# The output product of an attention and expert layer from 16-bit halves, and a new order of its neighbours

## Chip, core and metric

The kernel runs on one core of a Trainium2 chip, in one launch. The metric is the device time of that core in microseconds (us), the median of several runs.

## What is computed

For each of 16 sequences of 256 tokens and width 128, the reference adds three things: the input, a state-space branch and an attention and expert branch. Cut to what matters:

```python
xn = layernorm(x)
# branch 1: xf = depthwise_conv(xn); dt = sigmoid(xf @ dt_w.T + dt_b) * 0.099 + 0.001
#           s_t = exp(dt * A) * s_(t-1) + dt * xf * b;  y_t = sum_d s_t * c      (16 states per channel)
# branch 2:
h = layernorm(xn, ln_g, ln_b)
q, k, v = h @ Wq, h @ Wk, h @ Wv                      # 16 heads of 64
q, k = l2norm(q) * q_scale, l2norm(k) * k_scale
attn = softmax(causal(10 * q @ k.T))
out = concat_heads(attn @ v) @ Wo                     # (256 x 1024) @ (1024 x 128)
h = layernorm(out, ln_g, ln_b)
gate = softmax(h @ gate_w + gate_b)
moe = sum_e gate[e] * (gelu(h @ w1[e] + b1[e]) @ w2[e] + b2[e])      # 8 experts, 512 wide
result = x + y + layernorm(moe, ln_g, ln_b)
```

## The kernel before, in words

All engines run hand-written programs that are fixed when the kernel is built; semaphores join them. After a prologue (weights loaded and split, sequence 0 projected) each engine runs `body(i)` for the sequences i = 0 to 15, then a tail. A body has two halves.

**Pair steps k = 0 to 9.** The 16 heads go as 8 pairs p. TensorE forms the scores of pair k into the PSUM tile S2 (`scores`, L427), ScalarE takes their exponentials (`exps`, L716), GpSimd cuts the causal part (`select`, L875), and one step later TensorE weighs the values (`weigh` of pair k-1, L444) into the PSUM bank O[p % 2]. One more step later VectorE divides (`divide` of pair k-2: L1052, L1055), TensorE turns the quotient in the same bank (`turn_o`, L451), and at step k ScalarE copies the turned pair k-3 to `OT` (`copy_ot`, L722), which frees the bank: `weigh` waits for it by the semaphore `ot_done`. Beside that TensorE projects the next sequence's Q and K from 16-bit halves (`project`, three 512-column products L332 to L334 into a bank J; `project_v` in steps 8 and 9), ScalarE copies and squares them (L666, L668), VectorE sums the squares (L992) and runs the recurrence of branch 1 (`scan` L1148, `add_state` L1158), whose decays ScalarE makes (L728).

**Expert steps m = 0 to 9.** TensorE forms the output product (`output`, L460, float32: the turned pairs as stationary, Wo as moving operand), the experts of the sequence before (`expert_up`, L521 to L523 from 16-bit halves; `expert_down`, L539), turns the next sequence's Q and K (`turn_qk`, L369), whose high halves ScalarE writes (`high`, L689 to L693) and whose low halves VectorE (`low`, L1029 to L1034), and forms scores a first time for their maxima (`scores_for_max`, L387 and L391, into S2 too), which VectorE reduces (`maxima`, L1046). The maxima of four pairs at a time are turned (`turn_max`, L405) and copied (`copy_max`, L697), and `scores(i, 0)` waits for that copy. The gate of the sequence before is turned (L499) and copied (L1106) in step 1, in front of `gated_b2` (L505).

Each engine takes its instructions in the order of its program. That order is written out in the loops of `body`, by the step at which a helper is called; small tables (`TURN_AT`, `MAX_AT`, `O_AT`, `STATES`) say which part comes at which step. `WS` is 64: 16-bit halves of weights are of the weight times 64, and the copy of a result divides by it.

Of the kernel before, what the change touches and what calls it, by code (L numbers as in the profile page):

```python
# [14 lines left out]
P = 128  # L15
# [25 lines left out]
def build(nc, x, a_log, b, c, dt_w, dt_b, conv_w, conv_b, ln_g, ln_b, Wq, Wk, Wv, q_scale, k_scale,  # L41
          Wo, gate_w, gate_b, w1, b1, w2, b2, out):
    ctx = ExitStack()
    with ctx:
# [3 lines left out]
        def sem(name):  # L48
# [13 lines left out]
        wos = sb("wos", [P, HD // P, D])  # L62
# [59 lines left out]
        OT = sb("OT", [P, NP, SEQ])  # L122
# [44 lines left out]
        W132 = hid[:, :, :, :].rearrange("p r c n -> p (r c n)")  # L167
        sel32 = P32[:, :, :, :].rearrange("p r a n -> p (r a n)")[:, 0:8 * P].rearrange("p (h k) -> p h k", h=8)
# [14 lines left out]
            st_ready ex_done sel_done pv_done rr_done on_done ot_ready ot_done  # L183
# [10 lines left out]
         st_ready, ex_done, sel_done, pv_done, rr_done, on_done, ot_ready, ot_done,  # L194
# [121 lines left out]
        def _(pe):  # L316
# [137 lines left out]
            def output(s):  # L454

                pe.wait_ge(ot_done, (s + 1) * NP)
                pe.wait_ge(ex_done, (s + 1) * NP)
                for t in range(T):
                    for m in range(HD // P):
                        last = mm(S2[:, 0, t * P:(t + 1) * P], OT[:, m, t * P:(t + 1) * P],  # L460
                                  wos[:, m, :], start=(m == 0), stop=(m == HD // P - 1))
                last.then_inc(wo_ready, 1)
# [85 lines left out]
            def prologue():  # L548
# [28 lines left out]
                pe.wait_ge(d_wo, 16)  # L577

            def body(i, older, old, new, newer):
                for k in range(NP + 2):  # L580
                    if k < NP:
                        scores(i, k)
                    if k == 0:
                        turn_max(i, 1)
                    if 1 <= k <= NP:
                        weigh(i, k - 1, older)
                    if new and k < NP:
                        project(i + 1, k)
# [13 lines left out]
                for m in range(NE + 2):  # L602
# [18 lines left out]
                    if not new and m == 8:  # L621
                        turn_gate(i, 0)
                        expert_up(i, 0)
                    if old and 1 <= m <= NE:
# [7 lines left out]
                    if new and m == 8:  # L632
                        turn_max(i + 1, 0)
# [15 lines left out]
        def _(act):  # L649
# [53 lines left out]
            def copy_output(s):  # L703
                act.wait_ge(wo_ready, s + 1)
                from_one(act, o_tr, s)
                fn(z2[:, :, :].rearrange("p t d -> p (t d)"), S2[:, 0, 0:SEQ], ACT.Copy).then_inc(wo_copied, 1)
# [11 lines left out]
            def copy_ot(s, p):  # L718
# [3 lines left out]
                fn(OT[:, p, :], O[p % 2][:, 0:SEQ], ACT.Copy).then_inc(ot_done, 1)  # L722
# [23 lines left out]
            def prologue():  # L746
# [32 lines left out]
                for n in range(NL):  # L779
                    high(0, n)  # L780
                    if n in (1, 5):
                        copy_v(0, n // 4 * 2)
                        copy_v(0, n // 4 * 2 + 1)
                act.wait_ge(setup_vec, 4)
                with_gelu_and_tanh()
                step_tanh(0)
                with_exp_and_ln()
                copy_max(0, 0)

            def body(i, older, old, new, newer):  # L790
                for k in range(NP + 2):
                    if k >= 3:
# [5 lines left out]
                    if new and 1 <= k <= NP:  # L798
                        copy_raw(i + 1, k - 1)
                    if k < NP:  # L800
# [15 lines left out]
                for m in range(NE + 2):  # L816
# [17 lines left out]
                    if new and m == 9:  # L834
                        copy_max(i + 1, 0)
                if new:
                    with_exp_and_ln()

# [101 lines left out]
        def _(dve):  # L940
# [54 lines left out]
            def norm_step(s, half, n):  # L995
# [196 lines left out]
            def prologue():  # L1192
# [64 lines left out]
                for n in range(7, 10):  # L1257
                    g_step(1, n)
                step_inputs(0, 0)
# [14 lines left out]
            STATES = {0: (6,), 1: (7,), 2: (8, 9)}  # L1274

            def body(i, older, old, new, newer):
                for k in range(NP + 2):
                    if k >= 2:
# [28 lines left out]
                for m in range(NE + 2):  # L1307
                    if old and m == 2:
                        o_step(i - 1, 15)
                    if old and m >= 2:  # L1310
                        add_expert(i - 1, m - 2)
                    if new and m == 0:
                        scan(i, 6)
                        low(i + 1, 0)
                        low(i + 1, 1)
                        norm_step(i + 1, 1, 1)
                        norm_step(i + 1, 1, 2)
                        norm_step(i + 1, 1, 3)
                        add_state(i, 6)
                    elif 2 <= m <= NE:  # L1320
                        for d in STATES.get(m, (m + 7,)):
                            scan(i, d)
                            add_state(i, d)
# [3 lines left out]
                    if old and m == 1:  # L1327
                        o_step(i - 1, 14)
# [3 lines left out]
                    if m == 1:  # L1332
                        if not new:
                            scan(i, 6)
# [62 lines left out]
```

## Time and profile before

| | |
|---|---|
| median of 3 runs | 1180.96 us (1180.76 to 1180.98) |
| the profiled execution | 1181.25 us, of which its span is 1179.5 us |
| granted TensorE clock, mean over the span | 0.977 |
| chain that ended last | PE 77%, ACT 12%, DVE 6%, issue 4% |
| busy share of GpSimd | 23% |

PE is TensorE's products and PEld its weight loads, DVE is VectorE, ACT ScalarE, POOL GpSimd. Times in a timeline are us from the span's start, first the start and then the duration, with the count of records in a row; a float32 product leaves two records. Products overlap, so the duration of one is longer than the distance from its start to the next one's. A wait is idle time of an engine, with the instruction that ended it; a wait for several things is put down to the last. A group's mean is over instructions of one shape.

### The profile page before, as it was taken

The page shows a single profiled execution, that of the slowest core. Times are in us where ns is not written, and L with a number is a line of the kernel's source. Part 1 is how long each engine was busy: PE and PEld are TensorE (multiplying, and loading weights), DVE is VectorE, ACT ScalarE, POOL GpSimd, SP SyncE. Part 2 cuts the span into 40 slices and gives each one's busy share as a digit, 9 for nine tenths or more (in the row PEclk, how much of TensorE's full clock was granted, in tenths as well). Part 3 has the DMA queues.
Part 4 walks back from the last instruction along what each step waited for, and adds up shares of the span by engine and source line. Part 5 has one row for each costly group of instructions (what it writes and reads, how often), then busy time and mean ns, then how long its engine had stood idle before and what let it go on. Part 6 is the DMA issues. An engine that isn't in the chain of part 4 may idle for free.

```text
span 1179.5 us, 27543 instructions
## 1 busy us (share of the span) xinstructions
PE 1106.3 (94%) x10435; PEld 920.3 (78%) x10435; DVE 960.0 (81%) x2576; ACT 784.9 (67%) x1772; POOL 268.3 (23%) x324
## 2 busy tenths in 40 slices
PE   4885999999999999999999999999999999999997
PEld 1563788887878888787887878788787888878897
DVE  7779778797987879788797988879798787978773
ACT  5582867758486675858667586766848677584753
POOL 2040312313041231313214041221404123130200
PEclk9795999999999999999999999999999999999999
DMA  6001000000000000000000000000000000000000
GB/s 201 6 1 41 6 1 15 2 11 6 6 11 1 15 2 6 10 6 11 1 15 2 6 10 6 11 1 13 4 6 11 1 15 1 7 6 1 10 2 9
DMA packets 18722, 14.60 MB, mean 12 GB/s; under 512 B 2408, under 2 KB 16160, under 8 KB 18592
## 3 DMA queue, kind: packets, MB, share of 16 engines
q1 hardware_dynamic: 17680, 12.76, 3.6%
q8 instruction: 84, 1.38, 0.5%
q14 instruction: 46, 0.38, 0.1%
q10 hardware_dynamic: 912, 0.09, 0.1%
HBM read 10.75 MB, written 2.10 MB: 11 GB/s over the span
## 4 chain that ended last, share of the span: by engine, by line
PE 77%; ACT 12%; DVE 6%; issue 4%; POOL 0%; POOLq 0%; DVEq 0%; ACTq 0%
PE O L539 18%; PE O L444 14%; PE S L427 9%; PE U L522 4%; PE U L523 4%; PE U L521 4%; PE J L332 3%; PE J L334 3%; PE J L333 3%; PE J L369 3%; PE S L391 3%; PE S L387 2%; PE O L451 2%; ACT L656 2%; ACT hid L743 1%
## 5 line engine op out<-in xcount | busy, mean ns | idle before, releaser
L743 ACT ACTIVATE hid<-U,b1c 128x256 f32<-128x256 f32 x512 | 200.5, 474 | 180.7 <-PE U L523 180.5
L539 PE MATMUL O<-w2s,hid 128*128 128x128 f32 x2048 | 251.8, 276 | 0.0
L539 PEld LDWEIGHTS O<-w2s,hid 128*128 128x128 f32 x2048 | 238.6, 192 | 2.9
L444 PE MATMUL O<-Vx,P 128*128 128x66 f32 x1536 | 198.9, 280 | 16.6 <-ACT OT L722 16.6
L444 PEld LDWEIGHTS O<-Vx,P 128*128 128x128 f32 x1536 | 182.0, 192 | 33.2 <-issue 19.6
L1148 DVE TENSOR_TENSOR_SCAN st<-aexp,u 128x256 f32<-128x256 f32 x256 | 175.2, 684 | 2.3 <-ACT aexp L728 2.3
L867 POOL TENSOR_TENSOR raw<-raw,nr 128x512 f32<-128x512 f32 x120 | 124.6, 1062 | 136.3 <-DVE nr L1011 136.2
L875 POOL TENSOR_SCALAR_AFFINE_SELECT P<-P 128x512 f32<-128x512 f32 x128 | 87.6, 684 | 217.8 <-ACT P L716 217.8
L522 PE MATMUL U<-h2l,w1h 128*128 128x256 f16 x480 | 130.9, 273 | 0.0
L521 PE MATMUL U<-h2h,w1h 128*128 128x256 f16 x480 | 130.9, 273 | 0.0
L523 PE MATMUL U<-h2h,w1l 128*128 128x256 f16 x480 | 130.9, 273 | 0.0
L716 ACT ACTIVATE P<-S 128x768 f32<-128x768 f32 x128 | 103.6, 810 | 36.7 <-PE S L427 36.5
L1046 DVE TENSOR_REDUCE mxn<-S 128x2 f32<-128x256 f32 x248 | 125.8, 550 | 0.1
L855 POOL TENSOR_TENSOR orr<-ove,minus_half 128x2 f32<-128x2 f32 x16 | 11.2, 698 | 495.9 <-DVE ove L1069 495.9
L1158 DVE SCALAR_TENSOR_TENSOR y<-st,bc,y 128x256 f32<-128x256 f32 x240 | 116.9, 487 | 8.3 <-issue 0.3
L728 ACT ACTIVATE aexp<-dt,negA 128x256 f32<-128x256 f32 x256 | 116.9, 516 | 0.0
L1119 DVE SCALAR_TENSOR_TENSOR acc<-O,gate,acc 128x128 f32<-128x128 f32 x240 | 72.9, 345 | 31.3 <-PE O L539 29.3
L992 DVE TENSOR_REDUCE ssq<-sq 128x8 f32<-128x512 f32 x128 | 86.5, 676 | 1.6 <-ACT sq L668 1.6
L1029 DVE SCALAR_TENSOR_TENSOR QTl<-J,wcol,QTh 128x256 f16<-128x256 f32 x64 | 30.8, 481 | 65.7 <-ACT QTh L690 65.6
L666 ACT ACTIVATE raw<-J 128x512 f32<-128x512 f32 x128 | 76.2, 595 | 4.2 <-PE J L334 4.1
L668 ACT ACTIVATE sq<-J 128x512 f32<-128x512 f32 x128 | 77.7, 607 | 0.0
L369 PE MATMUL J<-ident,raw 128*128 128x128 f32 x512 | 70.6, 282 | 7.0 <-DVE QTl L1031 3.7
(193 smaller groups left out, 2153.3 us busy)
## 6 DMA issues: line engine op xcount, KB each, us to landing
xin<-in_L_attn_x SPq DMA_DIRECT2D x16, 128.0 KB, 2.1
xres<-in_L_attn_x SPq DMA_DIRECT2D x16, 128.0 KB, 2.1
hid<-in_L_ffn_w SPq DMA_DIRECT2D x2, 1024.0 KB, 6.4
out_dram<-fin SPq DMA_DIRECT2D x16, 128.0 KB, 1.8
raw<-in_L_ffn_Wq SPq DMA_DIRECT2D x1, 512.0 KB, 4.2
raw<-in_L_ffn_Wk SPq DMA_DIRECT2D x1, 512.0 KB, 6.3
raw<-in_L_ffn_Wv SPq DMA_DIRECT2D x1, 512.0 KB, 7.3
wos<-in_L_ffn_Wo SPq DMA_DIRECT2D x1, 512.0 KB, 11.2
```

Of the source, the lines that this page charges most:

```text
L427: last = mm(S2[:, a, kb * SEQ:kb * P + SEQ], keys, queries, start=(n == 0), stop=(n == 3), skip_group_check=True)
L444: last = mm(dst, P32[:, p % 3, a, c0:c0 + P], Vx[:, kb, 2 * p + a, :], start=(kb == 0), stop=(kb == t))
L521: mm(dst, w1h[:, f:f + P], hi[:, :], start=True, stop=False)
L522: mm(dst, w1h[:, f:f + P], lo[:, :], start=False, stop=False)
L523: last = mm(dst, w1l[:, f:f + P], hi[:, :], start=False, stop=True)
L539: last = mm(O[e % 2][:, t * P:(t + 1) * P], hid[:, e % 2, m, t * P:(t + 1) * P], w2s[:, e * FC + m, :], start=(m == 0), stop=(m == FC - 1))
L728: fn(aexp[:, d, :], dt[:, :], ACT.Exp, scale=negA[:, d:d + 1]).then_inc(a_done, 1)
L743: fn(hid[:, e % 2, f % FC, :], U[q % 2][:, m * SEQ:(m + 1) * SEQ], ACT.Gelu_apprx_tanh, bias=b1c[:, f:f + 1], scale=1.0 / WS).then_inc(gel ...
L867: nc.gpsimd.tensor_tensor(group, group, nr[:, j * 8:(j + 1) * 8].unsqueeze(2).broadcast_to([P, 8, DH]), ALU.mult).then_inc(unit, 1)
L1046: V.tensor_reduce(mxn[:, t, g, hh:hh + DH + 2:DH + 1], max_bank(s, p)[:, :, t * P:(2 * t + 1) * P], AX.X, ALU.max, negate=True).then_inc(m ...
L1148: V.tensor_tensor_scan(st[:, d % 2, :], aexp[:, d, :], u[:, :], 0.0, ALU.mult, ALU.add).then_inc(scan_done, 1)
L1158: V.scalar_tensor_tensor(y[:, s % 2, :], st[:, d % 2, :], bc[:, d:d + 1], y[:, s % 2, :], ALU.mult, ALU.add).then_inc(y_done, 1)
```

## The change

1. **The output product from halves.** `woh` and `wol` are 16-bit high and low halves of Wo times 64, made in the prologue from a float32 copy that is loaded into a part of `P32`; ScalarE writes the high half, VectorE the low one, and the first `copy_max` waits for it. `OT` becomes `OTh` and `OTl`: ScalarE's `copy_ot` writes the high half (semaphore `ot_hi`), and a new VectorE helper `low_o` writes the low half from the bank and the high half and raises `ot_done`. `output` forms three 16-bit products where one float32 product was; `copy_output` divides by 64.
2. **`project` in front of `weigh`** in pair steps 1 to 7.
3. **ScalarE's copy of pair 5** moves from step 8 to step 7, in front of the decays.
4. **`turn_max(i + 1, 0)`** moves in front of the last `expert_down`, and its copy behind the load of the table of exponentials.
5. **VectorE's order.** `low_o` stands first in pair steps 3 to 9, and for pair 7 first in expert step 0. States 6 and 7 are both in expert step 0, in front of the low halves of Q and K, state 8 in step 1, 9 in step 2. The copy of the turned gate in step 1 moves in front of the low halves.

```diff
...
-        wos = sb("wos", [P, HD // P, D])
+        woh = sb("woh", [P, HD // P, D], F16)
+        wol = sb("wol", [P, HD // P, D], F16)
...
-        OT = sb("OT", [P, NP, SEQ])
+        OTh = sb("OTh", [P, NP, SEQ], F16)
+        OTl = sb("OTl", [P, NP, SEQ], F16)
...
+        wos = P32[:, :, :, :].rearrange("p r a n -> p (r a n)")[:, 1024:1024 + HD].rearrange("p (c n) -> p c n", n=D)
...
                 for t in range(T):
+                    dst, q = S2[:, 0, t * P:(t + 1) * P], slice(t * P, (t + 1) * P)
                     for m in range(HD // P):
-                        last = mm(S2[:, 0, t * P:(t + 1) * P], OT[:, m, t * P:(t + 1) * P],
-                                  wos[:, m, :], start=(m == 0), stop=(m == HD // P - 1))
+                        mm(dst, OTh[:, m, q], woh[:, m, :], start=(m == 0), stop=False)
+                        mm(dst, OTh[:, m, q], wol[:, m, :], start=False, stop=False)
+                        last = mm(dst, OTl[:, m, q], woh[:, m, :], start=False, stop=(m == HD // P - 1))
...
+                    if new and k < NP:
+                        project(i + 1, k)
                     if 1 <= k <= NP:
                         weigh(i, k - 1, older)
-                    if new and k < NP:
-                        project(i + 1, k)
...
+                    if new and m == 8:
+                        turn_max(i + 1, 0)
                     if old and 1 <= m <= NE:
                         expert_down(i - 1, m - 1, (i + 1) * NP)
...
-                    if new and m == 8:
-                        turn_max(i + 1, 0)
...
-                fn(OT[:, p, :], O[p % 2][:, 0:SEQ], ACT.Copy).then_inc(ot_done, 1)
+                fn(OTh[:, p, :], O[p % 2][:, 0:SEQ], ACT.Copy).then_inc(ot_hi, 1)
...
+                act.wait_ge(wo_low, 1)
                 copy_max(0, 0)
...
-                    if k >= 3:
+                    if k >= 3 and k != NP:
                         copy_ot(i, k - 3)
...
+                    if k == NP - 1:
+
+                        copy_ot(i, NP - 3)
                     if k < NP:
                         decay(i, 2 * k)
                         decay(i, 2 * k + 1)
...
-                    if new and m == 9:
-                        copy_max(i + 1, 0)
                 if new:
                     with_exp_and_ln()
+                    copy_max(i + 1, 0)
...
+            def low_o(s, p):
+
+                dve.wait_ge(ot_hi, s * NP + p + 1)
+                if p == 0:
+                    from_one(dve, wo_ready, s)
+                V.tensor_tensor(OTl[:, p, :], O[p % 2][:, 0:SEQ], OTh[:, p, :], ALU.subtract).then_inc(ot_done, 1)
...
+                dve.wait_ge(wo_high, 1)
+                V.scalar_tensor_tensor(wol[:, :, :], wos, WS, woh[:, :, :], ALU.mult, ALU.subtract).then_inc(wo_low, 1)
                 step_inputs(0, 0)
...
                 for k in range(NP + 2):
+                    if k >= 3:
+                        low_o(i, k - 3)
                     if k >= 2:
                         divide(i, k - 2)
...
+                    if m == 0:
+                        low_o(i, NP - 1)
+                        for d in (6, 7):
+                            scan(i, d)
+                            add_state(i, d)
...
+                    if old and m == 1:
+                        o_step(i - 1, 14)
                     if new and m > 0 and m in TURN_AT:
                         low(i + 1, TURN_AT[m])
                         low(i + 1, TURN_AT[m] + 1)
-                    if old and m == 1:
-                        o_step(i - 1, 14)
```

How the instructions stand now. VectorE, pair step 6 and the head of step 7, before (st and y are a scan and its state, gl the gate's logits):

```order
L1052 RECIPROCAL rr<-O 128x4 [waits pv_done]
L1055 TENSOR_TENSOR On<-O,rr 128x256 [waits ot_ready,rr_done]
L992 TENSOR_REDUCE ssq<-sq 128x8 [waits qk_raw]
L1148 SCALAR_TENSOR_TENSOR st<-aexp,u 128x256 [waits y_done,a_done]
L1158 SCALAR_TENSOR_TENSOR y<-st,bc,y 128x256 [waits y_done,scan_done]
...
L1094 TENSOR_SCALAR gl<-gl,gm 128x8 [waits o_vec]
L1094 TENSOR_SCALAR gl<-gl,gm 128x8
L1052 RECIPROCAL rr<-O 128x4 [waits pv_done]
L1055 TENSOR_TENSOR On<-O,rr 128x256 [waits ot_ready,rr_done]
```

and after the change:

```order
L1030 TENSOR_TENSOR OTl<-O,OTh 128x256 [waits ot_hi]
L1070 RECIPROCAL rr<-O 128x4 [waits pv_done]
L1073 TENSOR_TENSOR On<-O,rr 128x256 [waits ot_ready,rr_done]
L1003 TENSOR_REDUCE ssq<-sq 128x8 [waits qk_raw]
L1166 SCALAR_TENSOR_TENSOR st<-aexp,u 128x256 [waits y_done,a_done]
L1176 SCALAR_TENSOR_TENSOR y<-st,bc,y 128x256 [waits y_done,scan_done]
...
L1112 TENSOR_SCALAR gl<-gl,gm 128x8 [waits o_vec]
L1112 TENSOR_SCALAR gl<-gl,gm 128x8
L1030 TENSOR_TENSOR OTl<-O,OTh 128x256 [waits ot_hi]
L1070 RECIPROCAL rr<-O 128x4 [waits pv_done]
L1073 TENSOR_TENSOR On<-O,rr 128x256 [waits ot_ready,rr_done]
```

The subtraction that waits for `ot_hi` stands in front of the division; the rest of the step is as it was.

TensorE, from the last scores of a pair step to the turn, before:

```order
L427 MATMUL S<-QTh,KTl 128x128 x2
L444 MATMUL O<-Vx,P 128x66 [waits ot_done,sel_done]
L444 MATMUL O<-Vx,P 128x66 x5
L332 MATMUL J<-wh,hTh 128x512 [waits qk_raw]
L333 MATMUL J<-wh,hTl 128x512
L334 MATMUL J<-wl,hTh 128x512
```

and after:

```order
L430 MATMUL S<-QTh,KTh 128x128 x2
L430 MATMUL S<-QTl,KTh 128x128 x2
L430 MATMUL S<-QTh,KTl 128x128 x2
L335 MATMUL J<-wh,hTh 128x512 [waits qk_raw]
L336 MATMUL J<-wh,hTl 128x512
L337 MATMUL J<-wl,hTh 128x512
L447 MATMUL O<-Vx,P 128x66 [waits ot_done,sel_done]
```

The projection stands between the scores and the weighing, with its wait for the bank J; the weighing is directly in front of the turn.

ScalarE, the end of step 7 and step 8, before:

```order
L668 ACTIVATE sq<-J 128x512 [waits qk_sum]
L728 ACTIVATE aexp<-dt,negA 128x256 x2
L711 ACTIVATE ge,gs<-gl 128x8 [waits o_vec]
L711 ACTIVATE ge,gs<-gl 128x8
L722 ACTIVATE OT<-O 128x256 [waits ot_ready]
L666 ACTIVATE raw<-J 128x512 [waits qk_ready]
```

and after:

```order
L673 ACTIVATE sq<-J 128x512 [waits qk_sum]
L728 ACTIVATE OTh<-O 128x256 [waits ot_ready]
L734 ACTIVATE aexp<-dt,negA 128x256 x2
L717 ACTIVATE ge,gs<-gl 128x8 [waits o_vec]
L717 ACTIVATE ge,gs<-gl 128x8
L671 ACTIVATE raw<-J 128x512 [waits qk_ready]
```

The copy of pair 5 now stands in front of the decays and of the gate's exponentials.

## Rows read from the trace of the kernel before

**Rows 1.** The page, part 1: busy us (share) xinstructions of each engine.

```profile
...
PE 1106.3 (94%) x10435; PEld 920.3 (78%) x10435; DVE 960.0 (81%) x2576; ACT 784.9 (67%) x1772; POOL 268.3 (23%) x324
...
```

**Rows 2.** TensorE's waits: engine, line, waited for: us in total, times, longest us.

```profile
...
PE O L444 <- ACT OT L722: 16.6, 17, 1.1
PE S L387 <- DVE mxn L1046: 11.4, 6, 3.1
...
PE S L427 <- ACT mT L697: 8.5, 15, 0.6
...
PE O L505 <- DVE gateT L1106: 2.8, 14, 0.2
...
```

**Rows 3.** Timeline, TensorE, output: start us, us, line, op, xcount.

```profile
...
708.17 3.74 PE L460 MATMUL S<-wos,OT 128*128 128x128 f32 x32
...
713.21 0.40 PE L391 MATMUL S<-maskb,identb 128*128 128x128 bf16 x4
713.44 0.27 PE L521 MATMUL U<-h2h,w1h 128*128 128x256 f16 x1
...
```

**Rows 4.** Timeline, TensorE, pair steps 7 to 9 of the same body.

```profile
...
697.97 0.22 PE L427 MATMUL S<-QTh,KTl 64*128 64x128 f16 x2
698.12 1.55 PE L444 MATMUL O<-Vx,P 128*128 128x66 f32 x12
699.51 0.38 PE L332 MATMUL J<-wh,hTh 128*128 128x512 f16 x1
...
700.16 0.38 PE L451 MATMUL O<-ident,On 128*128 128x128 f32 x2
701.60 1.52 PE L444 MATMUL O<-Vx,P 128*128 128x66 f32 x12 [1.06 <-ACT OT L722]
...
704.26 0.38 PE L451 MATMUL O<-ident,On 128*128 128x128 f32 x2
...
705.77 0.38 PE L451 MATMUL O<-ident,On 128*128 128x128 f32 x2
...
```

**Rows 5.** Timeline, ScalarE, copies of turned pairs 3, 5 and 6.

```profile
...
694.53 0.36 ACT L722 ACTIVATE OT<-O 128x256 f32<-128x256 f32 x1
...
701.08 0.38 ACT L722 ACTIVATE OT<-O 128x256 f32<-128x256 f32 x1
...
704.95 0.38 ACT L722 ACTIVATE OT<-O 128x256 f32<-128x256 f32 x1
...
```

**Rows 6.** Timeline, VectorE, pair step 6 to the first low parts.

```profile
...
693.05 0.18 DVE L1052 RECIPROCAL rr<-O 128x4 f32<-128x4 f32 x1 [0.22 <-PE O L444]
...
696.28 1.35 DVE L1094 TENSOR_SCALAR gl<-gl,gm 128x8 f32<-128x8 f32 x2
697.55 0.17 DVE L1052 RECIPROCAL rr<-O 128x4 f32<-128x4 f32 x1
...
703.16 0.18 DVE L1052 RECIPROCAL rr<-O 128x4 f32<-128x4 f32 x1
...
705.65 0.68 DVE L1148 TENSOR_TENSOR_SCAN st<-aexp,u 128x256 f32<-128x256 f32 x1
708.81 0.48 DVE L1029 SCALAR_TENSOR_TENSOR QTl<-J,wcol,QTh 128x256 f16<-128x256 f32 x1 [2.48 <-ACT QTh L690]
...
```

**Rows 7.** Timeline, GpSimd, pair step 6.

```profile
...
696.57 2.04 POOL L867 TENSOR_TENSOR raw<-raw,nr 128x512 f32<-128x512 f32 x2
...
```

**Rows 8.** Groups by line and shape: out<-in shapes xcount | busy us, mean ns.

```profile
...
L1158 DVE SCALAR_TENSOR_TENSOR y<-st,bc,y 128x256 f32<-128x256 f32 x240 | 116.9, 487 | 8.3 <-issue 0.3
...
L988 DVE TENSOR_TENSOR hTl<-hT,hTh 128x256 f16<-128x256 f32 x16 | 6.6, 416 | 0.1
...
L1213 DVE SCALAR_TENSOR_TENSOR wl<-raw,wh 128x1024 f16<-128x1024 f32 x3 | 3.6, 1215 | 0.0
...
```

**Rows 9.** Timeline, TensorE, the edge between two bodies.

```profile
...
675.19 0.38 PE L405 MATMUL J<-ident,mxn 128*128 128x128 f32 x2
676.14 0.29 PE L427 MATMUL S<-mT,sel 64*128 64x256 bf16 x2 [0.56 <-ACT mT L697]
...
```

More of the change, by code:

```diff
@@ L182, in build @@
             m_ready mx_done mt_ready mt_done
-            st_ready ex_done sel_done pv_done rr_done on_done ot_ready ot_done
+            st_ready ex_done sel_done pv_done rr_done on_done ot_ready ot_hi ot_done wo_high wo_low
             wo_ready wo_copied o_vec o_root o_act o_tr o_gate o_gT o_b2
@@ L193, in build @@
          m_ready, mx_done, mt_ready, mt_done,
-         st_ready, ex_done, sel_done, pv_done, rr_done, on_done, ot_ready, ot_done,
+         st_ready, ex_done, sel_done, pv_done, rr_done, on_done, ot_ready, ot_hi, ot_done, wo_high, wo_low,
          wo_ready, wo_copied, o_vec, o_root, o_act, o_tr, o_gate, o_gT, o_b2,
@@ L576, in prologue @@
                 pe.wait_ge(d_w2, 16)
-                pe.wait_ge(d_wo, 16)
+                pe.wait_ge(wo_low, 1)
             def body(i, older, old, new, newer):
@@ L705, in copy_output @@
                 from_one(act, o_tr, s)
-                fn(z2[:, :, :].rearrange("p t d -> p (t d)"), S2[:, 0, 0:SEQ], ACT.Copy).then_inc(wo_copied, 1)
+                fn(z2[:, :, :].rearrange("p t d -> p (t d)"), S2[:, 0, 0:SEQ], ACT.Copy, scale=1.0 / WS
+                   ).then_inc(wo_copied, 1)
             def gate_exps(s):
@@ L783, in prologue @@
                         copy_v(0, n // 4 * 2 + 1)
+                act.wait_ge(d_wo, 16)
+                fn(woh[:, :, :], wos, ACT.Copy, scale=WS).then_inc(wo_high, 1)
                 act.wait_ge(setup_vec, 4)
@@ L1273, in _ @@
             SCAN_AT = {1: 0, 3: 1, 5: 2, 6: 3, 8: 4, 9: 5}
-            STATES = {0: (6,), 1: (7,), 2: (8, 9)}
             def body(i, older, old, new, newer):
                 for k in range(NP + 2):
+                    if k >= 3:
+                        low_o(i, k - 3)
                     if k >= 2:
@@ L1311, in body @@
                         add_expert(i - 1, m - 2)
+                    if m == 0:
[3 more added lines that the diff above has]
+                            add_state(i, d)
                     if new and m == 0:
-                        scan(i, 6)
                         low(i + 1, 0)
                         low(i + 1, 1)
[L1316 to L1323, printed above, removed]
+                        for n in range(1, 4):
+                            norm_step(i + 1, 1, n)
+                    if 2 <= m <= NE:
+                        scan(i, m + 7)
+                        add_state(i, m + 7)
+                    if old and m == 1:
+                        o_step(i - 1, 14)
                     if new and m > 0 and m in TURN_AT:
@@ L1332, in body @@
                     if m == 1:
-                        if not new:
-                            scan(i, 6)
-                            add_state(i, 6)
-                        scan(i, 7)
-                        add_state(i, 7)
+                        scan(i, m + 7)
+                        add_state(i, m + 7)
                     if newer and m == 5:
```

## The prediction

> **What bounds the kernel now.** I read three views in this order. The page's busy line [rows 1]: TensorE is busy 1106.3 us of the span (94%), VectorE 960.0 us (81%), ScalarE 67%. Then TensorE's waits [rows 2]: about once a body it stands still in front of a weighing (L444, 16.6 us in 17 waits, for ScalarE's copy L722), in front of the first scores (L427, 8.5 us in 15, for the copied maxima L697) and at L505 (0.2 us each). Then the timelines of one steady body [rows 3 to 7, 9]. The reader is to see that TensorE's row is nearly gapless, that VectorE idles only where it waits for TensorE (0.22 us in front of the division at 693.05, none in front of the one at 697.55), and that VectorE keeps the order of its program. So a us taken from TensorE's row or its waits is a us of the body, unless VectorE then delivers late. All times below are on the clock of that body; "late" is against it.
>
> **The output product.** 32 records take 3.74 us from first start to last end, 0.112 us each, together 3.58 us [rows 3]. They become 48 with 16-bit operands and 128 columns. The nearest row of this kind is L391 (128x128, 16 bits): four from 713.21 to 713.44, 0.058 us each [rows 3], so 48 take 2.8 us: 0.8 us less. Bounds: the three 512-column products of a projection take 0.65 us [rows 4], 0.054 per 128 columns, which would give 2.6; 0.112 us, no gain per record, 5.4. I take 0.058, because it is a run of the same shape.
> The Trainium skill ("TensorE: Matmul & The Clock Gate", on the sustained spacing of weight load and product pairs) speaks against this edit: about 81 ns each at 128 columns. By that figure 48 records would take 3.9 us, a little more than before.
>
> **Low halves on VectorE.** Each of the 8 pairs gets one subtraction 128x256 to 16 bits, behind ScalarE's copy. L988 has that shape: 416 ns [rows 8]; 8 per body add 3.3 us of VectorE. What matters is where they stand. In pair step k the low half of pair k-3 now stands in front of the division of pair k-2, so VectorE's whole step waits for the copy, which waits for the turn on TensorE at the end of step k-1. The weighing of pair k-1 needs this low half, since it frees the bank O.
>
> **Step 6 and 7.** ScalarE's copy of pair 3 runs from 694.53 to 694.89 [rows 5]. The low half then ends near 695.3 and the division of pair 4 starts at 695.25 instead of 693.05 [rows 6]: 2.2 us late. VectorE's step 6 takes 697.55 - 693.05 = 4.50 us without idle, of which 1.35 us are the two small L1094, which run beside the GpSimd instructions that begin at 696.57 [rows 6, 7]. So the low half of pair 4 starts at 699.75 and ends at 700.2. The weighing of pair 6 started at 698.12 before; behind the projection (699.51 to 700.16, 0.65 us) it would start at 698.77 [rows 4]. It now starts at 700.25, **a new wait of 1.5 us**, and the turn of pair 5, 1.34 us behind, at 701.6 instead of 700.16: 1.4 us late. Bounds: with L1094 free of charge the wait would be 0.1 us; if both L1094 each lose to a GpSimd instruction (half of 2.04 us [rows 7]) it is up to 2.2 us. I take the row's value.
> The Trainium skill ("GPSIMD Engine Reference", the table on SBUF interfaces) says that VectorE and GpSimd share interfaces, with contention for some VectorE instructions; the 1.35 us agree with it.
>
> **Projections in front of the weighing.** From the last scores to the weighing it is 0.15 us (697.97 to 698.12) where two such products need 0.055; from the weighing to the projection 1.39 us for 12 records of 0.112 [rows 4]. A 512-column product hides the next weight load (700.16 follows at the row's own spacing), so the new order saves about 0.1 us per step, in the five steps 2 to 6 that no wait decides: -0.5. Bounds 0 and -1.0. It also covers the low half in steps 3 to 6: scores and projection are 1.4 us, while copy and low half are through 1.4 us behind the turn, some 1.1 us after the step begins. In step 7 the cover is gone, as above.
>
> **The last weighing (pair 7).** Before: turn of pair 5 at 700.16, copy 701.08 to 701.46 behind the decays, weighing at 701.60 [rows 4, 5]. Now the copy stands in front of the decays and starts about 0.54 us behind the turn's start (0.38 us of its records and 0.15 of handover, an estimate; pair 6 shows 0.69), ends at 0.92, the low half at 1.37, the weighing starts at 1.5 against 1.44: **the repair and the low half cancel**, +0.1. The decays, the gate's exponentials and the raw copy now stand behind it; I cost that at nothing, since the weighing and the first value projection (1.34 and 0.65 us) cover them; without that cover it is the 0.9 us by which they start later than before at most.
>
> **The turn of pair 7.** Before, the division of pair 7 was over long before (it started at 703.16 [rows 6]). Now it stands behind the low half of pair 6: turn of pair 6 at 704.26, copy 704.95 to 705.33, low half, division at 705.7, quotient at 706.3, turn at 706.4 instead of 705.77 [rows 4, 5]: +0.6. Bounds 0.4 and 0.9 (half of the copy's delay behind the two Vx copies either way).
>
> **First expert steps.** VectorE's step 9 took 705.65 - 703.16 = 2.49 us; begun at 705.7 it ends at 708.2. Then the low half of pair 7 (0.34) and two scans and two states, 0.68 us [rows 6] and 487 ns [rows 8] long, 2.2 us with their overlap: QTl (L1029) starts at 710.8 instead of 708.81 [rows 6]. The output could end at 708.17 + 0.6 + 2.8 = 711.6, but the next turns of Q and K need the low parts, which end at 711.7 and 712.3: 0.35 us of the 0.8 is given back, -0.45. The gate's copy, now in front of the low parts, ends L505's wait: 0.2 us shown [rows 2] and some 0.15 of restart, -0.35.
>
> **Body's edge.** The maxima are turned in front of the last expert product, ScalarE copies them behind its table load. The scores started at 676.14, 0.95 us behind L405's 675.19, whose two records take 0.38 [rows 9]: -0.6. The select of pair 0 stands behind the root that VectorE feeds late (it adds the last expert 0.3 us later), so 0.2 is lost again at the first weighing: -0.4.
>
> **Sum per steady body:** -0.4 - 0.5 + 1.4 + 0.1 + 0.6 - 0.45 - 0.35 = **+0.4 us**, 14 bodies +5.6. The ends: in the prologue the low half of Wo, 128x1024, 1215 ns on VectorE [rows 8], holds back the first maxima: +1.2. The first body's expert half, where TensorE waits for VectorE (11.4 us at L387 [rows 2]), gets more VectorE work in front: +1. The last body has no projections, so each weighing waits about 0.3 us for its low half in six steps and the turn of pair 7 0.4, less 0.8 of output: +1.5. Together +3.7. Against the profiled execution's own 1181.25 us that makes 1190.6; the median of the runs is 1180.96, 0.3 below it, so I forecast **1190.3 us**, +0.8%.
>
> **Rivals.** (A) VectorE is not late in step 7, the side on which it gets faster: the place is the low half of pair 4, and the point from which it decides is whether it ends before 698.8, which needs step 6 of VectorE in about 3.1 us instead of 4.5. For it: 1.35 us of these are contention that can fall elsewhere. Against: the division of pair 5 had no idle in front of it even before. Without the 1.4 the body gains 1.0 us: 1181 - 14 + 3.7 = 1170.6; if the turn of pair 7 and the QTl are in time too, 2.0 us: 1157. Chance 0.22. (B) The GpSimd instructions, which now begin right where L1094 stands, hold both: 0.6 us more per body, 1199. Chance 0.20. (C) The records of the new output come at 0.081 us, as a rate between the two rows above: 1.1 us more than I take, of which 0.35 is hidden behind the late low parts, 0.75 x 14: 1201. For it: each has its own weight load, and the loads of the old form set the old spacing (192 ns each in pairs). Chance 0.06. This is also the time that the Trainium skill's figure ("TensorE: Matmul & The Clock Gate") would give. (D) The change does not do what it says in sum: gains and new waits cancel within the 0.2% (2.4 us) that a measurement of this kernel can tell from no change: 1181. Chance 0.10. My forecast's own case, 1184 to 1196, has 0.42.
>
> **How the numbers follow.** Slower: 0.42 + 0.20 + 0.06 = 0.68; same 0.10; faster 0.22. The range leaves out the far part of A (0.1) and the far ends of B and C (0.1): 1172 to 1203.
>
> **What would show each step.** In the profile after: the output's records near 0.058 us; a wait of TensorE at the weighing for VectorE's low half, twice a body, the first near 1.5 us in step 7, the second near 1.1; one at the turn of pair 7 for the quotient, near 0.6; the wait of the scores for mT gone; a steady body 0.4 us longer than before. I am wrong if the weighing of pair 6 doesn't wait, or if VectorE shows idle time in front of the low half of pair 4; then A holds.

## The result, and the profile after

The kernel with the change takes **1251.88 us** (median of 4 runs, 1250.86 to 1253.02), the kernel before on the same chip 1180.97: a ratio of 1.060, 95% interval 1.058 to 1.062. The sign is the forecast one. The size is not: the text said 1190.3, at most 1203. The page of the profile after:

```profile
span 1249.1 us, 28201 instructions
...
PE 1147.7 (92%) x10691; PEld 935.5 (75%) x10691; DVE 1023.0 (82%) x2705; ACT 787.4 (63%) x1773; POOL 260.8 (21%) x324
...
PEclk9895899898989989899998989989898998989799
```

The span is 69.6 us longer than before, and TensorE has 41 us more of busy time than in [rows 1], though the output product became shorter. The clock row says why to look further: here 8s stand among the 9s all through, while the same row of the kernel before is

```profile
PEclk9795999999999999999999999999999999999999
```

The waits, in us in total, times, longest:

```profile
DVE OTl L1030 <- ACT OTh L728: 114.6, 82, 3.7
...
PE O L447 <- DVE OTl L1030: 45.6, 34, 2.0
...
PE J L372 <- DVE QTl L1049: 3.9, 3, 3.4
```

L447 is the weighing (L444 before). Its wait for ScalarE's copy [rows 2] has become one for VectorE's low half, twice a body. Now the timeline of one steady body, TensorE from step 7 to the output (steady bodies are those after the first and before the last):

```profile
362.88 0.38 PE L337 MATMUL J<-wl,hTh 128*128 128x512 f16 x1
365.27 1.52 PE L447 MATMUL O<-Vx,P 128*128 128x66 f32 x12 [2.01 <-DVE OTl L1030]
366.63 0.39 PE L454 MATMUL O<-ident,On 128*128 128x128 f32 x2
368.04 2.80 PE L447 MATMUL O<-Vx,P 128*128 128x66 f32 x12 [1.02 <-DVE OTl L1030]
370.63 0.63 PE L335 MATMUL J<-wh,hTh 128*128 128x512 f16 x1
...
377.83 0.22 PE L464 MATMUL S<-woh,OTh 128*128 128x128 f16 x1
377.88 0.22 PE L465 MATMUL S<-wol,OTh 128*128 128x128 f16 x1
```

The two waits are the predicted ones. What follows is not: twelve products that took 1.52 us take 2.80, and the next 512-column product 0.63 us instead of 0.38. The windows of the same stretch (from start to end, length, then the busy time of PE, PEld, DVE, ACT and POOL; behind them PEclk, the granted clock as a share of 2.4 GHz, and two numbers on DMA):

```profile
349.00:365.20 16.20, 14.26 (x157) 11.05 (x153) 14.38 (x39) 14.21 (x31) 6.00 (x8) 1.00 0.04 11
365.20:367.60 2.40, 1.75 (x14) 1.54 (x14) 1.16 (x4) 0.55 (x2) 2.17 (x3) 1.00 0.00 0
367.60:374.50 6.90, 6.46 (x23) 4.31 (x24) 3.08 (x10) 3.45 (x11) 0.00 (x0) 0.51 0.00 0
374.50:380.00 5.50, 5.50 (x66) 4.76 (x65) 5.32 (x13) 4.30 (x9) 0.00 (x0) 1.00 0.00 0
```

From 367.6, while the second wait is still on, to 374.5 TensorE runs at 1.2 GHz. Such a stretch of 6.8 or 10.2 us stands in every body; over the trace I add up 181.8 us at the lower level, 54.0 in the kernel before, all but 2.8 of those ahead of the second body. The body (start of one output to the next) is 73.3 to 74.7 us long, 74.0 in the mean, 69.7 before.

VectorE and GpSimd in front of the first wait:

```profile
362.97 1.83 DVE L1112 TENSOR_SCALAR gl<-gl,gm 128x8 f32<-128x8 f32 x2
364.71 0.41 DVE L1030 TENSOR_TENSOR OTl<-O,OTh 128x256 f16<-128x256 f32 x1
```

```profile
362.73 2.04 POOL L878 TENSOR_TENSOR raw<-raw,nr 128x512 f32<-128x512 f32 x2 [1.70 <-DVE nr L1022]
```

The two small subtractions (L1094 before, 1.35 us) take 1.83 us: both lie beside a GpSimd multiplication, and each ends 0.03 us behind the end of one (363.79 and 364.80 against 363.77 and 364.77). VectorE's low half follows without idle time. The body's edge:

```profile
412.28 1.95 PE L544 MATMUL O<-w2s,hid 128*128 128x128 f32 x16
414.17 0.28 PE L430 MATMUL S<-mT,sel 64*128 64x256 bf16 x2
```

The first scores follow the expert product directly; the wait of [rows 9] is gone.

### The profile page after: what moved, and what is told of

It reads as the page before. It is cut to its first block, busy times and chain, and to the rows that moved or that the text cites. A ratio compares the mean times of both kernels' runs of the same rounds, so it can differ in the third digit from the quotient of the medians.

```text
span 1249.1 us, 28201 instructions
## 1 busy us (share of the span) xinstructions
PE 1147.7 (92%) x10691; PEld 935.5 (75%) x10691; DVE 1023.0 (82%) x2705; ACT 787.4 (63%) x1773; POOL 260.8 (21%) x324
## 3 DMA queue, kind: packets, MB, share of 16 engines
q8 instruction: 86, 1.41, 0.5%
## 4 chain that ended last, share of the span: by engine, by line
PE 72%; DVE 13%; ACT 7%; issue 6%; POOL 2%; POOLq 0%; DVEq 0%; ACTq 0%
PE O L544 17%; PE O L447 13%; PE S L430 5%; PE U L526 4%; PE U L527 4%; PE U L528 4%; PE J L372 4%; PE S L394 3%; PE J L335 3%; PE S L390 3%; PE J L336 2%; PE J L337 2%; PE O L454 2%; DVE st L1166 1%; DVE gl L1112 1%
## 5 line engine op out<-in xcount | busy, mean ns | idle before, releaser
L447 PEld LDWEIGHTS O<-Vx,P 128*128 128x128 f32 x1536 | 209.7, 213 | 80.4 <-issue 65.6
L447 PE MATMUL O<-Vx,P 128*128 128x66 f32 x1536 | 215.3, 296 | 48.0 <-DVE OTl L1030 45.6
L1166 DVE TENSOR_TENSOR_SCAN st<-aexp,u 128x256 f32<-128x256 f32 x256 | 182.2, 712 | 2.2 <-ACT aexp L734 2.2
L1030 DVE TENSOR_TENSOR OTl<-O,OTh 128x256 f16<-128x256 f32 x128 | 53.9, 421 | 114.7 <-ACT OTh L728 114.6
L886 POOL TENSOR_SCALAR_AFFINE_SELECT P<-P 128x512 f32<-128x512 f32 x128 | 82.6, 646 | 207.3 <-ACT P L722 207.3
L335 PE MATMUL J<-wh,hTh 128*128 128x512 f16 x188 | 83.9, 446 | 3.8 <-DVE hTl L999 2.8
L728 ACT ACTIVATE OTh<-O 128x256 f16<-128x256 f32 x128 | 49.0, 383 | 56.2 <-PE O L454 56.1
L336 PE MATMUL J<-wh,hTl 128*128 128x512 f16 x188 | 81.2, 432 | 0.0
```

The lines of the kernel that those rows point to most:

```text
L335: mm(dst, hi, wh[:, w0:w0 + 512], start=True, stop=False)
L447: last = mm(dst, P32[:, p % 3, a, c0:c0 + P], Vx[:, kb, 2 * p + a, :], start=(kb == 0), stop=(kb == t))
L1166: V.tensor_tensor_scan(st[:, d % 2, :], aexp[:, d, :], u[:, :], 0.0, ALU.mult, ALU.add).then_inc(scan_done, 1)
```

## Experiments

The theory after the result: the waits for late low halves cost about what the sum said, and the rest is TensorE's clock, which falls at them. The rivals: the halves cost by themselves, or the new orders do.

### 1. Both waits filled with products of no use

Their results are overwritten; they only keep TensorE busy where it would wait.

```diff
+                for _ in range(3 * extra):
+                    mm(J[j % 2][:, :], hTh[:, t * P:(t + 1) * P], wh[:, 0:512], start=True, stop=True)
...
-                        project(i + 1, k)
+                        project(i + 1, k, 3 if k == 7 else 0)
+                    if new and k == NP:
...
+                        for w0 in (2 * HD, 2 * HD, 2 * HD, 2 * HD):
+                            mm(J[0][:, :], hTh[:, t0], wh[:, w0:w0 + 512], start=True, stop=True)
                     if 1 <= k <= NP:
                         weigh(i, k - 1, older)
```

> The changed kernel with idle TensorE time filled: nine 512-column products whose result is overwritten in front of the projection of step 7 (1.95 us), and four in front of the weighing of step 8 (0.86 us). Theory (waits, then the clock): the waits for the low halves cost about 3 us a body by themselves, and TensorE's clock falls to 1.2 GHz behind them for 7 to 10 us, which costs as much again. With TensorE busy in those places the low stretches vanish, though it does 2.8 us more work per body: 1195 to 1210 us, granted clock back near 0.97. Rival (the clock falls for another reason, such as the 16-bit output product): clock stays near 0.93 and the time at 1250 us or above.

Measured: 1206.95 us, ratio 1.022 (1.019 to 1.024). **More work on TensorE, and 45 us less time.** Windows over the same two steps:

```profile
349.00:358.50 9.50, 9.42 (x88) 6.83 (x87) 8.68 (x22) 6.95 (x16) 4.96 (x7) 1.00 0.01 3
358.50:362.00 3.50, 3.34 (x24) 2.31 (x24) 2.47 (x8) 2.52 (x9) 0.86 (x1) 1.00 0.00 0
```

No steady body has a stretch at 1.2 GHz (65.6 us left in all, at both ends), and the body is 70.95 us long. The products fill the places of the waits, so those are still paid for. So of the 4.25 us by which the changed body is longer, 3.0 are the clock; 1.25 is what the waits cost beyond what the moves and the shorter product save.

### 2. Only the second wait filled

The last four products of the edit above stay, in front of the weighing in step 8; the nine in step 7 are gone, and its wait of 2.0 us is back.

> The change with the four products of no use in front of the weighing in step 8 only; the wait of 2.0 us in step 7 stays. If TensorE's clock falls for the two waits together: it stays up here and the time is that of the run with both waits filled, 1200 to 1215 us. Rival (the wait of 2.0 us is enough by itself): the stretches at half speed stay in every body, 1230 to 1250 us.

Measured: 1234.65 and 1244.49 us, ratio 1.049 (1.039 to 1.059). Windows of two bodies:

```profile
351.00:361.80 10.80, 8.79 (x96) 6.69 (x95) 9.66 (x27) 8.75 (x20) 4.86 (x7) 1.00 0.01 2
361.80:365.20 3.40, 3.40 (x15) 2.51 (x15) 1.19 (x4) 1.23 (x5) 1.53 (x2) 0.50 0.00 0
422.00:433.40 11.40, 9.41 (x102) 7.23 (x102) 10.26 (x27) 9.94 (x22) 5.41 (x7) 1.00 0.01 3
433.40:443.70 10.30, 10.28 (x39) 7.70 (x40) 4.06 (x11) 3.44 (x11) 2.13 (x3) 0.50 0.01 2
```

The wait of 2.0 us alone lowers the clock in 9 of the 14 bodies ahead of the last, for 3.4 or 10.2 us (bodies of 72.2 and some 75 us); the others are 71 us long, as in experiment 1. The two times lie in the rival's range, though not every body falls as it had said: one such wait is enough, mostly, and with the second every body falls.

### 3. The halves alone

The output product from halves and the low halves, with projections, turns of the maxima, copies and VectorE's order as before.

```diff
-                    if new and k < NP:
-                        project(i + 1, k)
                     if 1 <= k <= NP:
                         weigh(i, k - 1, older)
+                    if new and k < NP:
+                        project(i + 1, k)
...
```

> The 16-bit output product and VectorE's low halves alone; every order as in the kernel before. Theory: without the projection between scores and weighing every weighing waits some 0.3 us, step 7 about 2.1 to 2.8 us, step 8 1.6 us, and the clock falls as in the changed kernel: 1270 to 1290 us. Rival (the halves are harmless and the new orders did the harm): below 1190 us.

Measured: 1304.19 us, ratio 1.104 (1.102 to 1.106), above the range; most bodies are 78.4 us long. Without a projection in front, the weighing waits for its low half in six steps of a body, 4.6 us together: 2.38 in step 7, 1.02 in step 8 (less than the 1.6 expected), 0.26 to 0.38 in four others. 189.7 us of the trace are at 1.2 GHz:

```profile
PE O L447 <- DVE OTl L1028: 69.0, 96, 2.4
```

### 4. The orders alone

The change without its halves: the 32-bit product L460, no low halves, all moves kept.

```diff
-                    if k >= 3:
-                        low_o(i, k - 3)
...
-                        mm(dst, OTh[:, m, q], woh[:, m, :], start=(m == 0), stop=False)
-                        mm(dst, OTh[:, m, q], wol[:, m, :], start=False, stop=False)
-                        last = mm(dst, OTl[:, m, q], woh[:, m, :], start=False, stop=(m == HD // P - 1))
+                        last = mm(S2[:, 0, t * P:(t + 1) * P], OT[:, m, t * P:(t + 1) * P],
+                                  wos[:, m, :], start=(m == 0), stop=(m == HD // P - 1))
```

> All new orders, but the output product in float32 and no low half. Theory: the orders gain 0.6 us at the body's edge, 0.5 by the projections in front, 0.9 at the last weighing and 0.35 at the gate's copy, 14 to 15 times: 1145 to 1155 us, clock as before. Rival (an order does harm, say the copy of pair 5 in front of the decays): 1175 us or more.

Measured: 1160.97 us, ratio 0.983 (0.980 to 0.986), in two groups: 1157.0 and 1157.2, 1164.7 and 1164.9. The steady body is 68.0 us long: **the moves save 1.7 us a body, the halves cost that and 4.25 more.** The expected 2.35 us a body were too good. One part can be read: the copy of pair 5 was to give 0.9 us at the last weighing, and TensorE's wait there went from 1.06 to 0.56. The two groups of times are the matter of experiment 10.

### 5. The gate's steps 9 to 13 a step later

```diff
-            O_AT = {1: (5,), 4: (6, 7), 5: (8,), 6: (9, 10, 11), 8: (12, 13)}
+            O_AT = {1: (5,), 4: (6, 7), 5: (8,), 7: (9, 10, 11), 9: (12, 13)}
...
```

ScalarE's exponentials of the gate go with them, from step 7 to 8.

> The changed kernel with the gate's three small VectorE steps moved from pair step 6 to 7, its exponentials on ScalarE from 7 to 8 and the two steps behind them from 8 to 9. Theory: VectorE's step 6 falls from 5.3 to about 3.3 us, the low half of pair 4 is nearly in time (wait under 0.5 us instead of 2.0), one wait of 1.1 us is left, which did not bring the clock down in the kernel before: 1170 to 1190 us, clock near 0.97. Rival (the small steps only move the delay, since VectorE is late everywhere): above 1230 us.

Measured: 1199.45 us, ratio 1.015 (1.012 to 1.019), above the range, but 52 us under the change. The wait in step 7 is gone, the one in step 8 is what it was in the change. From the turn of pair 5 to the last weighing the rows are:

```profile
351.61 0.39 PE L454 MATMUL O<-ident,On 128*128 128x128 f32 x2
352.03 0.38 ACT L728 ACTIVATE OTh<-O 128x256 f16<-128x256 f32 x1 [0.58 <-PE O L454]
352.45 0.42 DVE L1030 TENSOR_TENSOR OTl<-O,OTh 128x256 f16<-128x256 f32 x1
353.02 1.64 PE L447 MATMUL O<-Vx,P 128*128 128x66 f32 x12 [1.02 <-DVE OTl L1030]
354.46 0.63 PE L335 MATMUL J<-wh,hTh 128*128 128x512 f16 x1
```

The low half starts as the copy ends, so VectorE, with the gate now in front of it, isn't late: the weighing stands 1.41 us behind the turn, as in the change, where VectorE had been idle for 1.21 us. This wait of 1.0 us, as long as the one of the kernel before in this place (1.06 us [rows 4]), goes with 3.4 us at 1.2 GHz in 8 of the 14 bodies ahead of the last; the theory had counted on the clock staying up, and that put the time above the range.

### 6. The same, with the low half behind the division and the sums

In VectorE's pair steps `low_o` now follows `divide` and `qk_sums`.

> The change with the gate's steps 9 to 13 a step later (as in the run before) and, in the pair steps, VectorE's low half behind the division and the sums. Theory (VectorE lacks time, not order): the wait at the turn for the quotient (12.4 us) goes, the wait at the weighing for the low half (17.3 us) grows by as much; 1190 to 1215 us, no better than 1199. Rival (only the order of these steps is wrong): both waits shrink and the time falls to 1165 to 1180 us.

Measured: 1207.81 and 1213.06 us, ratio 1.025 (1.022 to 1.028). The order within VectorE's step is not the fault: no better than 5, as the theory had it. The wait at the turn is gone, the one at the weighing is 24.7 us instead of 17.3.

### 7. Projections in front, on the kernel before

```diff
-                    if 1 <= k <= NP:
-                        weigh(i, k - 1, older)
                     if new and k < NP:
                         project(i + 1, k)
+                    if 1 <= k <= NP:
+                        weigh(i, k - 1, older)
```

> The kernel before with the projections in front of the weighed values and nothing else. Theory: the weighing's idle time for GpSimd's masking goes, 0.4 to 0.6 us a body; 1170 to 1177 us. Rival (the idle time only moves to the turn or the projection): 1179 to 1183 us.

Measured: 1184.64 us, ratio 1.003 (1.002 to 1.005): slower, outside of both. The bodies alternate: 69.1, 70.8, 69.1, 70.8 us. One of each, first the weighing in step 8 and the product behind it:

```profile
352.19 1.52 PE L444 MATMUL O<-Vx,P 128*128 128x66 f32 x12 [1.15 <-ACT OT L722]
353.55 0.38 PE L332 MATMUL J<-wh,hTh 128*128 128x512 f16 x1
...
421.31 1.89 PE L444 MATMUL O<-Vx,P 128*128 128x66 f32 x12 [1.15 <-ACT OT L722]
423.00 0.63 PE L332 MATMUL J<-wh,hTh 128*128 128x512 f16 x1
```

and the windows behind these weighings:

```profile
353.20:356.60 3.40, 3.40 (x22) 1.91 (x22) 3.22 (x8) 2.11 (x5) 0.00 (x0) 1.00 0.00 0
...
422.30:425.70 3.40, 3.40 (x12) 1.83 (x12) 2.84 (x7) 0.60 (x1) 0.00 (x0) 0.50 0.03 7
```

The same program, the same wait of 1.15 us: in one body the clock stays, in the next it falls for 3.4 us, seven times ahead of the last body, 139.95 us apart. In a body where it stays the new order saves 0.6 us, which is what the theory said; where it falls the body is 1.7 us longer than its neighbour, and the gain is more than lost.

### 8. The edge and the gate's copy, on the kernel before

```diff
+                    if new and m == 8:
+                        turn_max(i + 1, 0)
                     if old and 1 <= m <= NE:
                         expert_down(i - 1, m - 1, (i + 1) * NP)
...
+                    if old and m == 1:
+                        o_step(i - 1, 14)
                     if new and m > 0 and m in TURN_AT:
                         low(i + 1, TURN_AT[m])
                         low(i + 1, TURN_AT[m] + 1)
```

(the copy of the maxima also goes behind the table load, as in the change).

> The kernel before with the turn of the maxima one place earlier at the body's end, their copy behind the table load, and the copy of the gate's transpose in front of the low halves; nothing else. Theory (terms of the sum: 0.4 and 0.35 us a body): 1168 to 1172 us, if the clock stays up. Rival (only what the trace shows as waits before, 0.2 us for the gate and 0.56 for the maxima, less what moves on to the next wait): 1174 to 1180 us.

Measured: 1181.0 us, ratio 0.9996 (0.9987 to 1.0005); the body is 0.1 us shorter. TensorE's waits for the maxima and the gate are gone, and in their place stands a new one:

```profile
PE O L444 <- POOL P L874: 12.2, 14, 1.1
```

The scores come earlier, GpSimd's masking (which stands behind the root, and that waits for VectorE) does not, and without a projection between the two the weighing of pair 0 waits 0.85 us for it. In experiment 4, where the projection stands between them, the list has this wait once, in the last body, which has no projection:

```profile
PE O L444 <- ACT OT L722: 9.0, 16, 0.6
...
PE O L444 <- POOL P L877: 1.1, 1, 1.1
```

### 9. Waits mended, with and without the halves

To 5 are added: the values' first projection in front of the last weighing, and ScalarE's copy of pair 6 between the first two copies of the values.

```diff
+                    if new and k == NP:
+                        project_v(i + 1, 0)
                     if 1 <= k <= NP:
                         weigh(i, k - 1, older)
...
                         copy_v(i + 1, 2 * k - 16)
+                        if k == NP:
+                            copy_ot(i, NP - 2)
                         copy_v(i + 1, 2 * k - 15)
```

> The change with the gate's steps 9 to 13 a step later, the values' first projection put in front of the last weighing in step 8, and ScalarE's copy of pair 6 put between the first two copies of the values. Theory (waits of TensorE for late low halves and the clock that falls behind them are the whole loss): the low half's wait in step 8 is filled with work that is due anyway, the clock stays up in most bodies; 1150 to 1175 us, level with or under the orders without the halves (1161). Rival (the halves cost by themselves, by VectorE's eight more operations a body): 1185 us or more.

> The same orders as in the mended kernel, with the output product in 32 bits as before and no low halves. Theory: the product from halves saves 0.8 us a body where nothing waits for it, so this kernel is 5 to 13 us above the mended one. Rival (the low halves on VectorE cost more than the product saves wherever they stand): it is 3 us or more below the mended one.

Measured: with halves 1171.45 us (1165.27 to 1171.89), ratio 0.991 (0.988 to 0.993); without them 1161.27 (1160.86 to 1172.81), ratio 0.984 (0.982 to 0.985). No steady body falls to 1.2 GHz; they are 68.25 and 68.1 us long. So the same halves that cost 91 us in the change (1251.9 against 1161.0 in experiment 4) cost 10 here, and 0.15 us in a steady body: of the 10 us 2.9 lie ahead of the first output and 1.8 in the first body. But the claim that they save 0.8 us a body fails. The product does get shorter; the waits of the kernel with halves give it back:

```profile
PE O L447 <- DVE OTl L1037: 7.6, 20, 1.0
PE J L372 <- DVE QTl L1056: 7.3, 16, 3.4
```

The second has two waits in the kernel before (3.7 us); 14 new ones of 0.27 us are the next turns, which wait for the low halves of the queries.

### 10. The last body

The profiled execution of the orders alone is one of the slower group (1164.85 us). It ends in a body of 69.9 us, the kernel before in one of 61.7. There are no projections in the last body, and GpSimd's masking is waited for in one piece:

```profile
1071.53 2.49 PE L444 MATMUL O<-Vx,P 128*128 128x66 f32 x12 [1.13 <-POOL P L877]
```

```profile
1060.00:1072.00 12.00, 10.55 (x115) 8.93 (x114) 10.15 (x34) 7.32 (x15) 1.83 (x3) 1.00 0.00 1
1072.00:1085.60 13.60, 13.60 (x91) 11.45 (x91) 6.31 (x17) 4.62 (x10) 2.86 (x5) 0.50 0.07 20
```

The edit puts products of no use in front of three waits of this body only, into the orders alone:

```diff
+                    if not new and k in (1, 8):
+                        fill(k % 2, 6 if k == 1 else 4)
                     if 1 <= k <= NP:
                         weigh(i, k - 1, older)
...
+                    if not new and k == 9:
+                        fill(0, 6)
                     if k >= 2:
                         turn_o(i, k - 2)
```

> The orders of the change alone (32-bit output product, no low halves), with the same products with no use in the last body only. Theory: the two groups of times of the orders alone, 1157 and 1165 us, differ by whether TensorE's clock falls in the last body, where GpSimd's masking is waited for 1.3 us; with that wait filled the times are 1150 to 1158 us and lie close together. Rival (the spread is from somewhere else): again values near 1157 and near 1165.

Measured: **1155.56 us** (1155.22 to 1155.70), ratio 0.978 (0.977 to 0.980), the fastest of all: one group of times, and a last body of 62.5 us. Against the slower group of experiment 4 that is 9 us, against the faster (1157.0 and 1157.2) 1.5; that the faster one kept its clock here is likely, but none of its executions was profiled. The same place:

```profile
1063.00:1076.00 13.00, 12.68 (x143) 10.30 (x141) 11.01 (x36) 8.49 (x16) 4.16 (x7) 1.00 0.05 13
```

### 11. All mends together, with the halves

The mended kernel with the fill of 10, the gate's steps 9 to 11 in step 8 (its exponentials in step 9), 12 and 13 in expert step 0, and the seventh scan behind the low halves of queries and keys.

```diff
+            O_AT = {1: (5,), 4: (6, 7), 5: (8,), 8: (9, 10, 11)}
...
+                            o_step(i - 1, 12)
+                            o_step(i - 1, 13)
+                        scan(i, 6)
+                        add_state(i, 6)
                         low(i + 1, 0)
                         low(i + 1, 1)
+                        scan(i, 7)
+                        add_state(i, 7)
```

> The mended kernel with three more moves: the gate's steps 9 to 11 from pair step 7 to 8 and 12 and 13 to expert step 0, the seventh scan of step 0 behind the low halves of queries and keys, and in the last body sixteen products of 512 columns with no use in front of three waits (they stand in for the projections that this body lacks). Theory: the waits left in a body of the mended kernel (0.54 us for the low half, 0.43 for the low half of the queries, 0.19 at the output) go for the most part, and in the last body the clock stays up (13.7 us at half speed before); 1150 to 1162 us, under both kernels. Rival (VectorE is full and each move only shifts a wait): 1165 us or more.

Measured: 1159.64 us (1158.98 to 1160.30), ratio 0.982 (0.980 to 0.983). It beats the kernel before and loses to 10 by 4.1 us, of which 3.7 lie ahead of the first output (83.1 against 79.5 us). The steady body is 68.0 us, to 0.1 us that of experiment 10, which has no halves. TensorE is busy 0.5 us less in it and waits 0.5 us more, 1.1 us against the 0.56 for ScalarE's copy that are left in experiment 10. The waits here, with the halves:

```profile
PE O L452 <- DVE OTl L1046: 7.3, 22, 0.4
PE S L395 <- ACT z L723: 6.3, 14, 0.5
...
PE J L335 <- ACT Vx L697: 3.9, 15, 0.3
```

VectorE is in time (it stands idle 1.21 us in front of that low half, waiting for ScalarE's copy of the turned pair). What is left is the chain from the turn over the copy and the low half to the weighing, and ScalarE: it copies the output (L723) behind its table load and four GELUs, so a product that ends sooner doesn't bring that copy forward. The last is read from the rows; no run moved that copy.

## Why the prediction was wrong

**The failed step is one that isn't in the sum: the granted clock.** The sum priced a wait as its length. The profile before shows PEclk at 1.00 in all steady bodies with a wait of 1.06 us in each, and I took the clock as given. In the change 6.8 to 10.2 us at 1.2 GHz go with the two waits of 2.0 and 1.0 us, 3.0 us per body beyond the waits (experiments 1 and 2), and the last body adds 7.9 us instead of 1.5 (experiment 10 shows the same fall there without halves). All the rivals missed it too.

The forecast was 9.3 us more, the profiled executions are 69.6 us apart. Of the 60.3 us between, 42 are the clock in the 14 bodies ahead of the last, 11 the waits in them beyond the sum, 6.4 the last body, and 1 the two ends.

The named terms, against what the runs show:

- Output records: 0.056 us apart, forecast 0.058: right. Rival C (0.081) is out for this shape. So is the time by the Trainium skill's figure ("TensorE: Matmul & The Clock Gate", the section "Back-to-back issue gap"), an estimate of 3.9 us for the 48 records; they took 2.84.
- Wait in step 7: 2.0 us of idle time; counted as the forecast did, by starts, 2.2 (the weighing could have followed the last product of the projection by 0.22 us, at 363.10, and starts at 365.27). Forecast 1.5, bound 2.2. The place and cause are right; the term is mis-sized, because both small subtractions fell beside a GpSimd instruction. That is what rival B said, at its price. With 2.2 the sum gives 0.4 + 0.7 = 1.1 us a body; experiment 1, without the clock's part, measures 1.25.
- Last weighing: it starts 1.41 us behind the turn of pair 5 (366.63 to 368.04), forecast 1.5: right.
- Turn of pair 7: experiment 1 waits 8.3 us in 16 times at this turn for the quotient, 0.5 each, forecast 0.6: right. In the change the slow clock hides most of it.
- Output's gain: 0.45 us forecast to be left. From the output to the first scores the changed kernel takes 36.34 us and the orders alone (experiment 4) 36.70, so 0.36 are left there: nearly right. The wait for the queries' low halves is 0.27 us in experiment 9, forecast 0.35; mending it only brings up the next (experiment 11). Over a whole body the halves keep nothing in kernels mended alike (experiment 9), as the low halves are waited for in steps 7 to 9.
- Projections in front: -0.5, measured -0.6 where the clock stays (experiment 7).
- Edge and gate: -0.75 together, measured -0.1 alone (experiment 8), as the masking is waited for instead. In the change the projection covers that wait, and the terms hold: all moves together give -1.7 (experiment 4), of which 0.5 are the wait that the copy of pair 5 shortens there, and my terms for the rest are -1.25. The copy's move was not run alone, so this split is by its wait.
- Prologue: first output 1.9 us later, forecast 1.2.
- A reading that was wrong, without weight in the sum: VectorE doesn't idle only for TensorE. [Rows 6] themselves have 2.48 us in front of the queries' low half, for ScalarE's high half.

## What to carry to other kernels

A wait of TensorE of one or two us may cost more than its length, since the engine can come out of it at half its clock: a body with the wait of 2.0 us is up to 4.4 us longer when the clock falls than when it stays (experiment 2), one with the wait of 1.15 us 1.7 us (experiment 7). Count a stretch at 1.2 GHz as a loss of its own, look at the granted clock of every stretch, and put work that is due anyway (a projection that is in no hurry) in front of the wait. Shortening TensorE's work pays only as far as the engines behind it are early; here VectorE had to give 3.3 us a body for 0.8 us, and its lateness, then ScalarE's, took them back. Measure moves together with what covers them: edge and gate alone were worth 0.1 us, the projections alone less than nothing, all with the copy's move 1.7 us a body.

## What the runs showed of the hardware that I had not expected

- A fall of the clock is not a function of the wait alone. At 1.15 us it came in every second body of experiment 7 and not in the others; at 1.06 us [rows 4] in no steady body of the kernel before, nor with 0.85 us at pair 0 besides (experiment 8); at 1.02 us in 8 of 14 of experiment 5; at 2.0 us in 9 of 14 of experiment 2; at 2.0 and 1.0 in all; at waits of 0.56 us and less (experiments 4, 9 and 11) in no steady body. What decides in a given body stays open: in experiment 7 the waits of two such bodies are alike, and the falls come at an even distance of 139.95 us, so it isn't chance.
- The two small subtractions of the gate (128x8 each) take 1.83 us in the change, where they lie inside two GpSimd multiplications, 0.95 in experiment 5, where the end of one and a masking run beside them, and 0.36 in experiment 11, where the last multiplication ends at 552.92, 0.16 us behind their start, and holds neither:

```profile
552.76 0.36 DVE L1128 TENSOR_SCALAR gl<-gl,gm 128x8 f32<-128x8 f32 x2
```
